# One 128-node span per tile in both segment sums, and the duplicate and degree work moved into the attention loop

## The reference, cut to what matters

```
h = relu(layernorm(x))
# 1 relational: one of 8 weight matrices for each edge
msg = (h @ W_r)[etype, src] / deg(dst);  M = segment_sum(msg, dst)
x = x + where(deg > 0, relu(0.2*h + 0.8*M), h)
# 2 attention
e = tanh([h[src], h[dst]] @ W_attn.T + b_attn) @ w_out
a = exp(e - segment_max(e, dst)[dst]);  x = x + segment_sum(a*h[src], dst) / segment_sum(a, dst)
# 3 Chebyshev, K = 3, gates z and h~
deg = segment_sum(edge_weight, src);  w = -deg^-.5[src] * edge_weight * deg^-.5[dst]
Tx1 = segment_sum(w*h[src], dst); Tx2 = 2*segment_sum(w*Tx1[src], dst) - h;  x = x + gates(h, Tx1, Tx2)
# 4 graph convolution
x = x + segment_sum(edge_weight * (h @ W)[src], dst) + b
```

## Time and profile before

| | |
|---|---|
| median of 3 runs | 2011.47 us (2008.94 to 2014.19) |
| span of the profiled execution | 2533.2 us |
| mean granted PE clock in it | 0.660 |
| busy: PE, DVE, POOL, ACT | 1374.4, 991.2, 1235.7, 200.8 us |

### The profile page before, as it was taken

The page is one execution under the profiler, slowest core; times in us unless marked ns, Lnnn a source line. Parts: engine busy times, 40 slices in busy tenths (PEclk is TensorE's granted clock), DMA queues, the critical chain, the costliest instruction groups (busy, mean ns, idle before and its releaser), DMA issues.

```text
span 2533.2 us, 28723 instructions
## 1 busy us (share of the span) xinstructions
PE 1374.4 (54%) x7844; PEld 1089.7 (43%) x7845; DVE 991.2 (39%) x2889; ACT 200.8 (8%) x390; POOL 1235.7 (49%) x1381
## 2 busy tenths in 40 slices
PE   4455555565621556566555651111111898879877
PEld 2455554554511456556555640000000898434423
DVE  7555554554604333334333440000000676300488
ACT  2000000000000111111111100000000111000200
POOL 1666666666672366565666677677777000000000
PEclk8766767677755555555555555555555898899989
DMA  5444343435200222222222200000000002988878
GB/s 165 150 155 153 120 152 118 150 121 168 65 1 0 68 63 66 65 62 64 66 66 64 66 21 0 0 0 1 0 0 0 0 0 103 353 335 353 326 295 336
DMA packets 154645, 272.07 MB, mean 107 GB/s; under 512 B 44030, under 2 KB 100154, under 8 KB 151546
## 3 DMA queue, kind: packets, MB, share of 16 engines
q1 hardware_dynamic: 111322, 229.57, 24.9%
q0 software_dynamic: 40064, 41.32, 6.6%
q10 hardware_dynamic: 3232, 0.82, 0.1%
HBM read 215.32 MB, written 56.29 MB: 107 GB/s over the span
## 4 chain that ended last, share of the span: by engine, by line
another core or an unknown queue 28%; PE 26%; issue 20%; DVE 14%; POOL 5%; DMA 4%; DVEq 1%; ACT 1%; SPq 1%; POOLq 0%; ACTq 0%
PE acc L987 10%; PE acc L1035 7%; POOL rings L736 5%; PE acc L1029 4%; DVE rings L1367 2%; DVE big L1826 2%; DMA big<-pairs_by_src 2%; DVE rings L1401 2%; DVE rings L1402 1%; DVE big L1391 1%; DMA rings<-local_rows 1%; PE acc L1009 1%; DMA relation_rows<-big 1%; DMA rings<-relation_rows,idx_ring 1%
## 5 line engine op out<-in xcount | busy, mean ns | idle before, releaser
L987 PE MATMUL acc<-rings 128*65 128x128 f32 x3328 | 576.1, 326 | 634.4 <-issue 459.6
L987 PEld LDWEIGHTS acc<-rings 128*65 128x65 f32 x3328 | 456.0, 168 | 709.4 <-issue 694.3
L736 POOL DMA_INDIRECT rings<-relation_rows,idx_ring x416 | 409.5, 984 | 281.9 <-issue 184.1
L736 POOL DMA_INDIRECT rings<-attention_rows,idx_ring x416 | 394.6, 948 | 305.1 <-issue 234.3
L1029 PE MATMUL acc<-attend_mem,rings 128*128 x1664 | 373.8, 411 | 266.2 <-issue 182.3
L1029 PEld LDWEIGHTS acc<-attend_mem,rings 128*128 128x128 f32 x1664 | 367.3, 328 | 273.0 <-issue 273.0
L753 POOL DMA_INDIRECT pairs_by_src<-fed_val,fed_idx x416 | 405.6, 975 | 149.4 <-issue 120.0
L1425 DVE TENSOR_SCALAR rings<-iota_bf,col_local,score 128x256 f32<-128x256 bf16 x416 | 139.4, 408 | 480.3 <-remote 371.8
L786 POOL DMA_INDIRECT big<-support_rows,ext_node x4 | 3.9, 963 | 450.6 <-DMA support_rows<-big 449.7
L1680 DVE TENSOR_TENSOR rings<-acc,rings 128x512 f32<-128x512 f32 x52 | 35.6, 684 | 352.0 <-remote 343.9
L1035 PE MATMUL acc<-big,attend_mem 128*64 128x512 f32 x700 | 163.0, 600 | 9.1 <-DMA big<-pairs_by_src 9.1
(11 more groups left out here) (279 smaller groups left out, 895.0 us busy)
## 6 DMA issues: line engine op xcount, KB each, us to landing
big<-pairs_by_src SPq DMA_DIRECT2D x54, 2048.0 KB, 12.5
pairs_by_src<-zeros SPq DMA_DIRECT2D x24, 1792.0 KB
big<-key_rows SPq DMA_DIRECT2D x52, 512.0 KB
rings<-local_rows SPq DMA_DIRECT2D x52, 256.0 KB
big<-pairs_by_src SPq DMA_DIRECT2D x12, 1024.0 KB, 12.3
rings<-relation_rows,idx_ring POOLq DMA_INDIRECT x416
pairs_by_src<-fed_val,fed_idx POOLq DMA_INDIRECT x416
rings<-attention_rows,idx_ring POOLq DMA_INDIRECT x416
```

Source lines behind the costliest of these rows:

```text
L736: pool.indirect_dma_start(ring[h][:, u, 0:width], None, table, bass.IndirectOffsetOnAxis(ap=idx_ring[h][:, u:u + 1], axis=0),).then_inc(ga ...
L987: m = pe.matmul(node_sums[:, bass.ds(at[u] * P + w * P, P)], rows[h][:, u, :], onehot[h][:, u, w * P:(w + 1) * P], start=False, stop=False ...
```

## The change

- **Sums.** The span of a tile begins at its first destination and holds 128 nodes instead of two blocks of 128. PSUM's eight banks each hold 512 nodes and overlap by 128, so that a span lies in one bank; `turn_nodes` adds the overlapping parts with seven more products. Each tile costs one product of 128 columns instead of two, and DVE's one-hots are 128 wide.
- **Relational one-hots by ACT.** relu(1 - |iota - position|), with eight Abs of 128 columns and one Relu of 1024 per half step (`window_hots`).
- **Duplicates** are written by every equal edge with the same sum to the same cell, so the dump addresses, the four extra columns and `indices` go. The first 64 tiles are done by DVE in the first 8 half steps of the relational loop (`early_dups`), from broadcasts of keys and weights. The other tiles, and the degrees of all of them, move into the attention loop (`take_dups`, `tile_hots`).
- **Look-up** by one product of 128 columns per tile, with both candidate rows as right side; DVE picks between them with `copy_predicated`. The transposed one-hot of a half step is one instruction of 1024 columns.
- **SP** broadcasts keys in the attention loop; the zeros are stored in 48 halves of 0.9 MB, paced by the gathers from the fifth iteration on. The attention broadcasts wait for the table's store.
- The inverse roots of the degrees are taken while the aggregation runs.

```diff
@@ gather, scatter (POOL)
-            scatter(0, EARLY)
+            scatter(0, EARLY, early_val[:, :], early_ready, EARLY // H, EARLY // H)
             gather("att", attention_rows, rows2, 2 * D, 1, 1)
-            pool.wait_ge(idx_ready, 2)
-            scatter(EARLY, T)
+            scatter(EARLY, T, dup_val[:, H:], dups_ready, EARLY // H + 5, 2 * IT + 1)
@@ ACT
+            def window_hots(it, h):
+                act.wait_ge(rows_free["rel"], it * 4 + 2 * h + 2)
+                for u in range(H):
+                    o = act.activation(onehot[h][:, u, :], iota_bf[:, 0:P], ACT.Abs, scale=-1.0,
+                                       bias=col_window[:, bass.ds(it * (2 * H) + (h * H + u), 1)])
+                o.then_inc(away_ready, 1)
+                act.wait_ge(away_ready, it * 2 + h + 1)
+                act.activation(onehot[h], onehot[h], ACT.Relu, scale=-1.0, bias=1.0).then_inc(onehot_ready["rel"], 1)
@@ add_up (PE)
                         for u in range(H):
-                            for w in range(2):
-                                m = pe.matmul(node_sums[:, bass.ds(at[u] * P + w * P, P)], rows[h][:, u, :],
-                                              onehot[h][:, u, w * P:(w + 1) * P],
-                                              start=False, stop=False, skip_group_check=True)
-                            if key == "rel":
-                                if u % (H // 2) == H // 2 - 1:
-                                    m.then_inc(rows_free[key], 1)
-                                m = pe.matmul(degree_bank[:, degree_at:degree_at + 3 * NB], onehot_lo[h][:, u, :],
-                                              hi_parts[h][:, u, :], start=False, stop=False, skip_group_check=True)
-                        if key == "rel":
-                            pe.wait_ge(dups_read, it * 2 + h + 2)
-                            for u in range(H):
-                                m = pe.matmul(dup_bank[:, u * 7:(u + 1) * 7], eq[h][:, u, :],
...
+                            m = pe.matmul(node_sums[:, bass.ds(at[u], P)], rows[h][:, u, :], onehot[h][:, u, :],
+                                          start=False, stop=False, skip_group_check=True)
@@ look_up (PE)
-                            for w in range(2):
-                                m = pe.matmul(work[2 + h][:, u * D:(u + 1) * D], onehot_t[h][:, w, u * P:(u + 1) * P],
-                                              there[:, w * D:(w + 1) * D], start=(w == 0), stop=False, skip_group_check=True)
+                            m = pe.matmul(found[h][:, u * 2 * D:(u + 1) * 2 * D], onehot_t[h][:, u * P:(u + 1) * P], there,
+                                          start=True, stop=True, skip_group_check=True)
                         m.then_inc(slot_free[key], 1)
+                        pe.wait_ge(hots_ready, it * 2 + h + 2)
+                        for u in range(H):
+                            pe.matmul(degree_bank, onehot_lo[h][:, u, :], hi_parts[h][:, u, :],
+                                      start=False, stop=False, skip_group_check=True)
+                        for u in range(H):
+                            m = pe.matmul(dup_bank[h][:, u, :], eq[h][:, u, :], parts_ring[h][:, u, :],
+                                          start=True, stop=True, skip_group_check=True)
+                        m.then_inc(degrees_added, 1)
@@ DVE
+            def tile_hots(it, h):
+                n = it * 2 + h
+                cols = bass.ds(it * (2 * H) + h * H, H)
+                dve.wait_ge(keys_here[h], (it + 1) * 16)
+                dve.tensor_tensor(eq[h], key_ring[h], key_cols[:, cols].unsqueeze(2).to_broadcast([P, H, P]),
+                                  ALU.is_equal).then_inc(keys_read, 1)
+                dve.wait_ge(hots_ready, n + 1)
+                dve.tensor_tensor(onehot_hi, iota_bank[:, 0:NB].unsqueeze(1).to_broadcast([P, H, NB]),
+                                  col_hi[:, cols].unsqueeze(2).to_broadcast([P, H, NB]),
+                                  ALU.is_equal).then_inc(hi_ready, 1)
+                dve.tensor_tensor(onehot_lo[h], iota_bank.unsqueeze(1).to_broadcast([P, H, P]),
+                                  col_lo[:, cols].unsqueeze(2).to_broadcast([P, H, P]), ALU.is_equal)
+                dve.wait_ge(hi_ready, n + 2)
+                dve.wait_ge(parts_ready, n + 1)
+                for k in range(3):
+                    o = dve.tensor_tensor(hi_parts[h][:, :, k * NB:(k + 1) * NB], onehot_hi,
+                                          parts_ring[h][:, :, k:k + 1].to_broadcast([P, H, NB]), ALU.mult)
+                o.then_inc(hots_ready, 1)
@@ score_step (DVE)
                     elif not last:
                         onehot_rows("att", local_here, it + 1, 0)
+                    take_dups(it, h)
+                    tile_hots(it, h)
                     dve.wait_ge(gathered["att"][h], (it + 1) * (16 * H))
                     dve.wait_ge(slot_free["att"], it * 2 + h + 3)
-                    dve.tensor_tensor(msg[h][:, :, :], work[2 + h][:, :].rearrange("p (t d) -> p t d", t=H),
-                                      rows2[h][:, :, 0:D], ALU.add).then_inc(bank_read, 1)
+                    dve.wait_ge(upper_ready, it * 2 + h + 1)
+                    both = found[h].rearrange("p (t w d) -> p t w d", t=H, w=2)
+                    dve.nop(nofuse=True)
+                    dve.copy_predicated(both[:, :, 0], upper_ring[h][:, :].unsqueeze(2).to_broadcast([P, H, D]), both[:, :, 1]
+                                        ).then_inc(picked, 1)
+                    dve.wait_ge(picked, it * 2 + h + 1)
+                    dve.tensor_tensor(msg[h][:, :, :], both[:, :, 0], rows2[h][:, :, 0:D], ALU.add).then_inc(bank_read, 1)
@@ SP
-            with sp.Fori(0, ZERO_STEPS) as it:
-                keys_step(it)
-                zero_step(it)
+            with sp.Fori(0, EARLY // (2 * H)) as it:
+                for h in range(2):
+                    early_step(it, h)
+                    zero_step(it, h)
+            with sp.Fori(EARLY // (2 * H), ZERO_STEPS) as it:
+                for h in range(2):
+                    sp.wait_ge(gathered["rel"][h], (it + 1) * (16 * H))
+                    zero_step(it, h)
...
+            sp.wait_ge(table_stored["att"], 16)
             broadcast_local("att", local_here)
```

More of the change, by code:

```diff
@@ L56, in gnn_kernel @@
     VB = N // P
+    SPAN = BANK - P
+    TOP = VB * P
+    SUM_BANKS = 8
+    assert SUM_BANKS * SPAN == TOP and SPAN % P == 0 and NODES == TOP + P
+    PER_SPAN = SPAN // P
     SLOTS = 6
@@ L885, in _ @@
             take_sums("rel")
[L887 to L889 removed]
+            std(1)
             take_turned(0, hT_att, range(NG), work)
@@ L977, in add_up @@
                         _, at = nc.values_load_multi_w_load_instructions(
-                            block_at[0:1, bass.ds(it * (2 * H) + h * H, H)], engines=[PE_ENGINE], min_val=0, max_val=NB - 1,
-                            skip_runtime_bounds_check_because="a node's block, below NB")
+                            sum_at[0:1, bass.ds(it * (2 * H) + h * H, H)], engines=[PE_ENGINE], min_val=0,
+                            max_val=SUM_BANKS * BANK - P, skip_runtime_bounds_check_because="a window's column, within a bank")
                         pe.wait_ge(onehot_ready[key], it * 2 + h + 1)
@@ L1015, in look_up @@
                 for h in range(2):
-                    pe.matmul(work[2 + h][:, :], zeros[:, 0:P], zeros[:, :], start=True, stop=True
-                              ).then_inc(slot_free[key], 1)
+                    for i in range(2):
+                        m = pe.matmul(found[h][:, i * BANK:(i + 1) * BANK], zeros[:, 0:P], zeros[:, :], start=True, stop=True)
+                    m.then_inc(slot_free[key], 1)
+                clear(product_bank)
+                clear(banks[3]).then_inc(degrees_added, 2)
                 with pe.Fori(0, IT) as it:
```

402 lines of the change are left out of this document (206 added, 196 removed).

## The result

The changed kernel takes 2023.68 us (median of 4 runs, 2022.47 to 2028.18) against 2012.45 for the kernel before: ratio 1.0067, 95% interval 1.0047 to 1.0086. It is slower by 11 us, where 1997 us and a gain were forecast. The range from 1940 to 2040 held the time, the sign was wrong.

A forecast was written before the change was run, and what follows sets the result against it. POOL's indirect DMAs were taken to set the end in all four loops. From 2011 us, minus 15 (relational gathers), plus 3 (start), minus 2 (scatters) gave 1997 us; own range 1985 to 2007, whole range 1940 to 2040.

The forecast's parts named there:

- the rebuilt plain run: POOL's path, us: start 58, relational gathers 520, scatters 83, attention gathers 520, late scatters 458, last layers 291; 81 unplaced.
- Rival B: Behind the attention loop: compute was already on the path by 52 us and the shorter sum cuts it, 1945 us; chance 0.20.
- what the prediction named last: Whole kernel: if the slow spells are plain-run work, halving PE's instructions gains far more than 50 us; POOL's pace doesn't count.
- Relational loop: Relational gathers: less DVE work beside POOL shortens a gather from 984 to 948 ns, a gain of 15 us.
- Start: Before the first loop: added short DVE instructions cost 3 us of the 58, bounds 0 and 6.
- Aggregation and scatters: Late scatters: the sum falls from 182 to 92 to 120 us, hidden; scatters beside narrower DVE work gain 2 us.
- Attention loop: Attention gathers: DVE's 9.1 us per half step stay under POOL's 10.0, gathers not slowed, so cost 0.
- rival A: Attention loop: DVE becomes the bound past 10.0 us per half step, kernel slower, 2039 us at 10.8; chance 0.23.
- Keys' broadcast: Attention loop: 0.5 MB per half step enter DMA queues with a share of 0.22; no cost charged.
- the term of 291: Layers 3 and 4 on POOL's path: 279 us from the trace plus an estimated 12 for the last part's load.
- Rival C: Aggregation: PE's clock stays low with half its work gone; time 1997 to 2005 us; chance 0.05.
- D: Whole kernel: nothing changes within what can be measured, 2011 + 1 us; chance 0.12.

The follow-up runs named there:

- the split kernel: Changed kernel, transposed one-hot of a half step as four tensor_scalars of 256 columns instead of one of 1024: 2013.38 us, ratio 1.0021; fourth chip 2488.22 us, 0.9759.
- the experiment: Changed kernel, but DVE makes the relational one-hots again, eight tensor_scalars of 128 columns per half step, ACT none: 2026.45 us, ratio 1.0059.

## Why the prediction was wrong

**What bounds the kernel: right, by a wrong reason.** On the three chips POOL's chain sets the end of all four loops. The terms of the rebuilt plain run against the trace: 58 measured as 59.5, 520 as 544.8, 83 as 91.3, 520 as 525.9, 458 as 483.4 and 291 as 300.3. So 75 of the unplaced 81 us are found: 25 in the relational loop (19.5 of them hold-ups of the gathers), 8 and 25 in the scatters, 6 in the attention loop, 1 at the start and 9 behind the last scatter. The other 6 are between this span and the median. Rival B needed 52 us as compute. But the sum of the aggregation ends at 1435.9 us, 268 us before the last scatter, and with half of its instructions gone the late scatters' stage stayed at 483 us. B is refuted on the three chips. But the step "I therefore read the slow spells as the recording's" was false. They occur in plain runs of the fourth chip, and there B's mechanism holds and what the prediction named last came true: the sum ends behind the last scatter, and the change gains 88 us, far more than POOL's pace tells. The price of 0.109 us in a free stretch was right: 182 us were told for the aggregation's sum and 184.8 measured, 92 to 120 for the halved one and 117 measured.

**Relational loop: right in size and route.** 15 us forecast, 14.2 measured and up to 24 in the other traces, by the route named (991 to 956 ns). The row it was taken from, 984 against 948, held. It was DVE's work that left. But the one-hots that are left to make, now by ACT, account for 1.7 us of it, as the experiment showed; the rest was the degrees' one-hots and the second block between them.

**Start: right.** +1.9 us against 3, inside 0 and 6. Zeros, ACT and PE in the loops: POOL waited for none of them above 6 us in a loop, as forecast. Aggregation and scatters: 0.4 us less instead of 2, which the traces can't tell from nothing.

**Attention loop: the failed step.** The DVE sum of 9.1 us was looked after with care, and DVE stayed under POOL's 10.0: 350.75 us busy in the loop of 543, where 430 were told (rival A is refuted on the three chips; copy_predicated took 0.70, the low bound). What failed is the sentence after it: "The attention gathers may be slowed from 948 to 984 ns by a busier DVE: 0 to +15 us; I take 0, since it is tensor_scalar that leaves this loop (eight of 256 columns become one)". The gather went to 970. Fewer instructions and less tensor_scalar time did not mean fewer hold-ups; a longer instruction did mean more. A gather that starts inside a long one stands until it ends, and one that has run for 0.3 to 0.5 us when it begins is caught too; with 0.75 us on end 44 of 416 are caught, with eight short ones 4. That is 10.8 us of the 17.2. The Trainium skill's rule in "SBUF — State Buffer", section "Who interferes with whom", says that the blocked engine waits for the whole instruction of the other; the trace agrees, with 1.38 instead of 0.94 us, and agrees too that tensor_tensor with an operand in PSUM doesn't block (0.94 inside L1449). The prediction cited the rule and left out the word "whole".

**Keys' broadcast "enter a loop of share 0.22": mis-sized.** The share was low and the term was taken as 0. It cost some 6 us where POOL pauses: 5.4 by the run with the broadcast cut down, and 6.4 in all beyond the gathers' own length. Why POOL pauses longer is argued, not shown. A share is an average; POOL's pauses are three moments.

**Duplicates: the step that wasn't taken.** The change's own line says that all equal edges write the same sum to the same cell. It was costed at nothing and not even listed. Its cost is 11 us of landing (10.5 to 12 in the stage), at the end of the scatters where the last load waits for it with nothing to hide it, and it comes from 123 edges which aren't in the graph. A landing for the last scatter was missing in the term of 291 as well (12 us were put down for the load, and the trace has 7.2 for the landing and 20 for the load and its issues).

Sum of the measured terms, 1.9 - 14.2 + 0.8 + 17.2 - 0.4 + 12.0 = +17.4, against the forecast 3 - 15 - 2 = -14. Without the same-cell writes and the long one-hot the changed kernel takes 1995.02 us, near the forecast of 1997, but that is in part luck: its attention loop is still 6 us longer than that of the kernel before (532.1 against 525.9), and the stretch from the last scatter on 6 us shorter (295.4 against 301.2), and neither was forecast. Rival C: the clock in the late scatters' stage went from 0.78 to 0.72, and in the rest from 0.91 to 0.90; the late scatters' stage kept its length, and the loss behind them is the landing's. D is refuted: the gain and the losses are each larger than 0.3%, and so is their sum.

The way that came out, slower, had a chance of 0.21, nearly all of it for rival A, which is not what happened. Two slips in the working changed nothing: the gain elsewhere is used up at 10.27 us per half step (14/52), not 10.35; and the chain between the loops is said to be at most 2 us short of 83 us and then, at 72, 11 short.

Not settled: why PE and DVE issue so slowly on the fourth chip while POOL issues indirect DMAs, and whether it is always so there.

## What to carry to other kernels

When one engine's short operations set the pace, look at the longest single instruction of the engine that can block it, not at the sum: the same work in pieces of 256 columns cost 0.5 to 2 us, in pieces of 1024 it cost 11 to 21 us. On the fourth chip the split kernel was the slower one, so measure where it will run. Before dropping a device that keeps scattered writes apart, count how many padding entries share one address, and where in the program their landing is awaited. And when a profiled execution is much longer than the plain runs, profile once more before calling any part of the trace an artefact.

## What the runs showed of the hardware

Some 123 writes of 4 bytes to one cell took 18.2 to 19.4 us to land where the same writes spread over 64 rows took 2.15, an estimate of 0.14 us for each write ((19.2 - 2.15) / 122). A tensor_tensor with both inputs in SBUF holds up a gather as a tensor_scalar does. The changed kernel's early duplicates show it:

```profile
85.92 1.23 DVE L1472 TENSOR_TENSOR big<-big 128x1024 f32<-128x1024 f32 x1 [2.19 <-DMA big<-weight_rows]
86.00 1.97 POOL L768 DMA_INDIRECT rings<-relation_rows,idx_ring  x1 [0.30 <-issue]
```

The gather took 1.97 us and ended 0.8 us after the tensor_tensor, as above behind the tensor_scalar; seven of the eight gathers that start inside L1472 were held, by 0.36 to 1.02 us. And one chip differs from another by a quarter of the time on this kernel: 2015 against 2552 us, with a ratio for the change of 1.007 beside the former kind and 0.967 on the latter.
